# Two output stores moved up in ScalarE's queue, in a pre-norm attention and mixture-of-experts block

## The chip, the cores and the metric

The kernel runs on one core of a Trainium2 chip. The metric is the device time of one execution in microseconds (us). Device times are given as the median of several executions; one further execution was recorded by the hardware profiler.

## The reference, cut to what matters

The input is 16 sequences of 256 tokens with 128 features (4096 tokens in all, float32).

```
x = x + linear_attention(layernorm(x))            # 16 heads, elu + 1 features
x = x + moe(layernorm(x)) + shared(layernorm(x))  # 16 experts, top 2, sigmoid gates
moe(z)    = sum over the 2 chosen experts of gate * down_e(silu(gate_e z) * up_e z)
shared(z) = down(silu(z @ sg) * (z @ su))         # hidden size 256
```

The output is the last x. In the kernel it is called X1: it holds x after attention, and the shared expert's output and both routed experts' outputs are added to it in place before it is stored.

## The kernel before, in words

Tokens are worked on in 8 quads of 512 tokens, or in 16 halves of 256 (a half is half of a quad). The kernel has three stages. The first does attention, the second layer norm and the routing for each quad, and scatters the normalised rows to a buffer in HBM sorted by expert. The second loops over 80 items of 128 sorted rows, runs each through its expert and scatters the result to `results` in HBM; the shared expert's work for halves 0 to 10 lies in and before this loop. The third stage, the tail, begins when the last item is done. It is written out without a loop, as one fixed list of instructions for each engine:

- SyncE (SP) waits for the last scatters and then issues ten loads of `results` into ZB (the loads `YL`, lines 368 and 370): quads 0 to 5 whole, 512 KB each, then halves 12 to 15, 256 KB each. Each has a semaphore of its own.
- TensorE (PE) does the shared expert's gate and up matmuls of halves 11 to 15 (`shared_gu`, line 1005) and its down matmuls (`shared_d`, line 1015). The gate matmuls of a half wait for VectorE's product of two halves before.
- ScalarE (ACT) does one silu for each of these halves (`shared`, line 508). Behind the last silu it issues the ten stores of the output (`out_v`): quads 0 to 5, 256 KB each (line 546), each behind a wait for that quad's sums (`c_out`), then halves 12 to 15, 128 KB each (line 549). Its queue is in order: an instruction behind a wait stays there until the wait is met. Its last instruction waits until all stores have landed (`s_out`).
- VectorE (DVE) multiplies silu and up (`shared_h`, line 849), adds the down output to X1 (`shared_add`, line 854), and adds the two experts' results to X1 (`total(q)` for a quad, lines 958 and 960; `total_half(i)` for a half, lines 967 and 969). The second of these two adds releases `c_out`.

The order on VectorE comes from a small table, `DUE = {3: (0,), 2: (1,), 1: (2, 3)}`, read at `HALVES - i`: total(0) stands behind the product of half 13, total(1) behind that of half 14, total(2) and total(3) behind that of half 15, and then total(4), total(5), the last shared_add and the four total_half. `HALVES` is 16, `WHOLE` is 6, and `AFTER`, the first half of the tail, is 11.

Of the kernel before, what the change touches and what calls it, by code (L numbers as in the profile page):

```python
# [20 lines left out]
SPQ = QTOK // SEQ  # L21
# [13 lines left out]
HALVES = TOKENS // HALF  # L35
# [7 lines left out]
WHOLE = 6  # L43
FIRST = 2
DONE_FIRST = 16
DUE = {3: (0,), 2: (1,), 1: (2, 3)}
# [28 lines left out]
def preln_block(nc, x, w_att, bo, w_ffn, consts, tokid, out):  # L75
# [15 lines left out]
    out_v = out.rearrange("(q b p j) c -> q p b (j c)", b=SPQ, p=P, j=2)  # L91

    with ExitStack() as ctx:
        def sb(name, shape, dt=F32):
            return ctx.enter_context(nc.sbuf_tensor(name, shape, dt))
# [4 lines left out]
        def sem(name):  # L100
            return ctx.enter_context(nc.semaphore(name))
# [7 lines left out]
        X1 = sb("X1", [P, NQ * QTOK])  # L109
# [167 lines left out]
        c_sum, c_out, s_out = sem("c_sum"), sem("c_out"), sem("s_out")  # L277
# [6 lines left out]
        def quad(t, q):  # L284
            return t[:, bass.ds(q * QTOK, QTOK)]
# [120 lines left out]
        def _(act):  # L406
# [97 lines left out]
            def shared(i):  # L504

                act.wait_ge(h_gu, count_of(i) + 1)
                wait(act, h_h, count_of(i) - 1)
                nc.scalar.activation(sh_s[place(i)], banks_of(i)[0], ACT.Silu).then_inc(h_silu, 1)
# [28 lines left out]
                    silu(ITEMS - 1, BODY - 1)  # L537


            for i in range(AFTER, HALVES):  # L540
                shared(i)


            for q in range(WHOLE):
                act.wait_ge(c_out, q + 1)
                act.dma_start(out_v[q], quad(X1, q).rearrange("p (b f) -> p b f", b=SPQ)).then_inc(s_out, 16)
            for i in range(2 * WHOLE, HALVES):
                act.wait_ge(c_out, i - WHOLE + 1)
                act.dma_start(out_v[i // 2, :, i % 2, :], X1[:, i * HALF:(i + 1) * HALF]).then_inc(s_out, 16)
# [804 lines left out]
```

## Time and profile before

| | |
|---|---|
| device time, median of 3 runs | 315.89 us (313.11, 315.89, 319.8) |
| device time of the profiled execution | 313.39 us |
| span of the profiled execution, first to last instruction | 311.5 us |
| granted TensorE clock, mean of the span | 0.893 |
| tail, from the last item's last VectorE operation to the end | 285.6 to 311.5 us |
| busy in the span: PE, DVE, ACT, POOL | 77%, 52%, 41%, 39% |

Positions are microseconds from the start of the span. The profiled execution's device time is 1.9 us longer than its span. An engine name with a q (ACTq, SPq) marks what the engine's instruction queue does itself, such as issuing a transfer; the duration of such a row is that of the issue, and the time from issue to landing is given apart.

### The profile page before, as it was taken

Reading aid. Unit: us, or ns where it says so; the run is one execution under the profiler, and the core shown is the slowest. Engines: PE = TensorE matmul, PEld = TensorE weight load, DVE = VectorE, ACT = ScalarE, POOL = GpSimd, SP = SyncE. Lnnn points to the kernel's source line nnn. Section 1 sums busy time; section 2 is a strip of 40 time slices with the busy share of each in tenths; the row PEclk is TensorE's granted clock in tenths of the full one; section 3 lists DMA queues with packets and bytes.
Section 4 is the critical chain, followed back from the end, with each engine's and each line's share of the span. In section 5 each row is a group of like instructions: output and inputs, shape, how many; then the busy total and the mean of one; then the engine's idle time right before and its main releaser. Section 6 shows DMA issues by size and latency. Waiting matters only on the chain.

```text
span 311.5 us, 5386 instructions
## 1 busy us (share of the span) xinstructions
PE 238.9 (77%) x1334; PEld 189.6 (61%) x1335; DVE 163.4 (52%) x759; ACT 126.6 (41%) x341; POOL 122.9 (39%) x132
## 2 busy tenths in 40 slices
PE   6999974779486859677988678777887967886960
PEld 2477753667365647335787666666776856764850
DVE  4778975364737462524444443453454444443496
ACT  2968771646361612140024444343444344341210
POOL 0000073717272727274400465446344444655000
PEclk9999997859687968796799999999799799996995
DMA  8999930101010101013923233232233232111794
GB/s 246 432 224 221 320 114 18 51 17 45 27 51 17 54 27 52 17 51 95 121 50 90 79 99 97 70 85 77 61 87 81 68 85 77 42 42 36 265 383 169
DMA packets 26842, 33.06 MB, mean 106 GB/s; under 512 B 4531, under 2 KB 21046, under 8 KB 26694
## 3 DMA queue, kind: packets, MB, share of 16 engines
q1 hardware_dynamic: 18934, 21.16, 23.9%
q0 software_dynamic: 4096, 8.46, 8.6%
q10 hardware_dynamic: 3792, 3.21, 4.1%
q8 instruction: 8, 0.13, 0.2%
q14 instruction: 12, 0.10, 0.1%
HBM read 15.74 MB, written 12.75 MB: 91 GB/s over the span
## 4 chain that ended last, share of the span: by engine, by line
PE 64%; issue 16%; DVE 9%; ACT 5%; another core or an unknown queue 4%; DMA 1%; DVEq 0%; ACTq 0%
PE pQ L1189 6%; PE pZ L1189 6%; PE pKVN L1045 6%; PE pN L1197 3%; PE pKVN L1197 3%; PE pN L1005 3%; PE pKVN L1005 3%; PE pKV L1015 3%; PE pT L1183 3%; PE pN L1096 3%; PE pN L1061 2%; PE pKV L1035 2%; PE pKVN L1204 2%; PE pZ L1079 2%
## 5 line engine op out<-in xcount | busy, mean ns | idle before, releaser
L383 POOL DMA_INDIRECT routed<-ZB,ROWS x64 | 61.5, 961 | 91.1 <-DVE ROWS L711 74.0
L400 POOL DMA_INDIRECT results<-Y x64 | 61.3, 957 | 73.4 <-DVE Y L843 54.0
L838 DVE SCALAR_TENSOR_TENSOR Y<-pN,XS,Y 128x128 f32 x40 | 14.0, 351 | 32.6 <-PE pN L1197 10.1
L838 DVE SCALAR_TENSOR_TENSOR Y<-pKVN,XS,Y 128x128 f32 x40 | 14.0, 351 | 31.2 <-PE pKVN L1197 10.4
L1189 PE MATMUL pQ<-WF,attT 128*128 x80 | 26.3, 411 | 4.9 <-ACT attT L498 3.3
L1189 PE MATMUL pZ<-WF,attT 128*128 x80 | 26.7, 416 | 3.1 <-issue 2.9
L498 ACT COPY attT<-pT 128x256 f32<-128x256 f32 (+1 forms) x42 | 15.2, 363 | 29.1 <-PE pT L1183 11.2
L498 ACT COPY attT<-pN 128x256 f32<-128x256 f32 (+1 forms) x41 | 15.1, 368 | 24.5 <-PE pN L1183 13.4
L1045 PE MATMUL pKVN<-WA,XNT 128*128 128x256 f32 x64 | 22.3, 509 | 0.0
L1105 PE MATMUL pZ<-chosen,tri 128*128 128x64 bf16 x8 | 1.6, 200 | 23.1 <-issue 22.7
L1045 PEld LDWEIGHTS pKVN<-WA,XNT 128*128 128x128 f32 x64 | 15.8, 258 | 3.4 <-ACT XNT L441 0.5
L1197 PEld LDWEIGHTS pKVN<-WF,attT 128*128 128x128 f32 x80 | 15.9, 200 | 2.3
L1197 PEld LDWEIGHTS pN<-WF,attT 128*128 128x128 f32 x80 | 15.8, 199 | 2.5 <-issue 0.2
L1189 PEld LDWEIGHTS pQ<-WF,attT 128*128 128x128 f32 x80 | 12.5, 196 | 7.0 <-issue 6.6
L655 DVE MAX8 top<-pZ 128x8 f32<-128x16 f32 x32 | 3.4, 169 | 25.3 <-remote 20.2
L1105 PEld LDWEIGHTS pZ<-chosen,tri 128*128 128x128 bf16 x8 | 0.8, 100 | 25.3 <-issue 25.3
L1197 PE MATMUL pKVN<-WF,attT 128*128 x80 | 16.2, 286 | 0.0
L1197 PE MATMUL pN<-WF,attT 128*128 x80 | 16.2, 285 | 0.0
L1183 PE MATMUL pT<-CN,att 128*128 128x128 f32 x40 | 11.7, 293 | 5.8 <-DVE att L830 5.8
L1183 PE MATMUL pN<-CN,att 128*128 128x128 f32 x40 | 11.6, 290 | 5.5 <-DVE att L830 3.8
L1180 PE MATMUL pT<-CN,XS 128*128 128x128 f32 x40 | 11.3, 282 | 5.8 <-issue 5.8
L1189 PEld LDWEIGHTS pZ<-WF,attT 128*128 128x128 f32 x80 | 12.3, 193 | 5.1 <-issue 4.5
(192 smaller groups left out, 569.8 us busy)
## 6 DMA issues: line engine op xcount, KB each, us to landing
XS<-routed SPq DMA_DIRECT2D x80, 65.0 KB
Y<-pad SPq DMA_DIRECT2D x1, 4160.0 KB
WF<-w_ffn SPq DMA_DIRECT2D x1, 3456.0 KB, 14.5
ZB<-results SPq DMA_DIRECT2D x6, 512.0 KB, 6.0
X<-x SPq DMA_DIRECT2D x8, 256.0 KB, 5.7
routed<-pad SPq DMA_DIRECT2D x25, 65.0 KB, 13.2
out<-X ACTq DMA_DIRECT2D x6, 256.0 KB, 2.2
routed<-ZB,ROWS POOLq DMA_INDIRECT x64
```

The lines of the kernel that those rows point to most:

```text
L383: nc.gpsimd.indirect_dma_start(routed, bass.IndirectOffsetOnAxis(ap=ROWS[:, q, t, k:k + 1], axis=0), Z[:, q, t, k, :], None).then_inc(scat ...
L400: nc.gpsimd.indirect_dma_start(results, bass.IndirectOffsetOnAxis(ap=Y[:, b * YROW + D:b * YROW + D + 1].bitcast(U32), axis=0), Y[:, b * Y ...
L498: nc.scalar.copy(xhT[:, j % 2, a:b, :], pXH[j % 2][:, a:b, :]).then_inc(s_xhT, 1)
L838: nc.vector.scalar_tensor_tensor(part, pY[j % 2], XS[:, j, D + 1:D + 2], part, ALU.mult, ALU.add).then_inc(s_y, 1)
L1005: l = nc.tensor.matmul(bank[:, f * HALF:(f + 1) * HALF], WF[:, w0 + f * P:w0 + (f + 1) * P], ZT[:, bass.ds(i * HALF, HALF)], start=True, s ...
L1015: l = nc.tensor.matmul(down_bank(i)[:, t * D:(t + 1) * D], sh_h[place(i)][:, f * HALF + t * P:f * HALF + (t + 1) * P], WF[:, F_SD + f * D: ...
L1045: i = nc.tensor.matmul(pKVN[:, t, :], XNT[:, q % 2, t * P:(t + 1) * P], WA[:, W_KV:W_KV + 2 * D], start=True, stop=True)
L1096: i = nc.tensor.matmul(pO[:, t * P:(t + 1) * P], attT[:, t * P:(t + 1) * P], WA[:, W_O:W_O + D], start=False, stop=(t == QUAD - 1))
L1180: i = nc.tensor.transpose(pXH[j % 2][:, 0, :], XS[:, j, 0:D], ident)
L1183: i = nc.tensor.transpose(pXH[j % 2][:, 1, :], h[:, (j - 3) % 2, :], ident)
L1189: nc.tensor.matmul(pGU[j % 2][:, 0:2 * EXP_DIM], xhT[:, j % 2, 0, :], WF[:, bass.ds(w, 2 * EXP_DIM)], start=True, stop=True).then_inc(s_gu, 1)
L1197: nc.tensor.matmul(pY[j % 2], xhT[:, (j + 3) % 2, 1, :], WF[:, 2 * EXP_DIM:][:, bass.ds(w, D)], start=True, stop=True).then_inc(s_D, 1)
```

## The change

The six stores of whole quads become a function `store(q)`. In the loop over the last silus, after the silu of half i, ScalarE now issues the stores that the same table names at `HALVES - i + 1`: for i = 14 the store of quad 0, for i = 15 that of quad 1. Those not yet issued follow behind the loop, as before. Each store keeps its wait for `c_out`, its size and its place among the stores. The number of instructions is the same; the only pair whose order changes is the store of quad 0 (with its wait) and the silu of half 15.

```diff
+            def store(q):
+                act.wait_ge(c_out, q + 1)
+                act.dma_start(out_v[q], quad(X1, q).rearrange("p (b f) -> p b f", b=SPQ)).then_inc(s_out, 16)
+
+            stored = 0
             for i in range(AFTER, HALVES):
                 shared(i)
-
-
-            for q in range(WHOLE):
-                act.wait_ge(c_out, q + 1)
-                act.dma_start(out_v[q], quad(X1, q).rearrange("p (b f) -> p b f", b=SPQ)).then_inc(s_out, 16)
+                for q in DUE.get(HALVES - i + 1, ()):
+                    store(q)
+                    stored = q + 1
+            for q in range(stored, WHOLE):
+                store(q)
```

## Rows read from the trace of the kernel before

**Rows 1.** Timeline, ScalarE: start, duration, line, tiles, idle before and its releaser

```profile
296.29 0.60 ACT L508 ACTIVATE rq<-pQ 128x512 f32<-128x512 f32 x1 [2.02 <-PE pN L1005]
298.91 0.60 ACT L508 ACTIVATE rk<-pKVN 128x512 f32<-128x512 f32 x1 [2.02 <-PE pN L1005]
298.91 7.37 ACTq L546 DMA_DIRECT2D out<-X  x6
307.03 2.73 ACTq L549 DMA_DIRECT2D out<-X  x4
```

**Rows 2.** Timeline, VectorE in the tail

```profile
295.95 0.69 DVE L960 TENSOR_TENSOR X<-X,ZB 128x512 f32<-128x512 f32 x1
...
297.85 0.68 DVE L958 TENSOR_TENSOR X<-X,ZB 128x512 f32<-128x512 f32 x1
...
298.57 0.69 DVE L960 TENSOR_TENSOR X<-X,ZB 128x512 f32<-128x512 f32 x1
...
299.54 0.69 DVE L849 TENSOR_TENSOR ek<-pN,rk 128x512 f32<-128x512 f32 x1 [0.27 <-ACT rk L508]
...
300.48 0.68 DVE L958 TENSOR_TENSOR X<-X,ZB 128x512 f32<-128x512 f32 x1
...
306.12 0.42 DVE L967 TENSOR_TENSOR X<-X,ZB 128x256 f32<-128x256 f32 x1
...
308.96 0.42 DVE L969 TENSOR_TENSOR X<-X,ZB 128x256 f32<-128x256 f32 x1
```

**Rows 3.** Store issues by line, ns min/median/max, then time to landing: lines 546, 549

```profile
L546 ACTq DMA_DIRECT2D out<-X x6: 377/378/482, 298.9 to 305.9; - x6
DMA to landing us min/median/max: 2.1/2.2/4.2
...
L549 ACTq DMA_DIRECT2D out<-X x4: 338/344/352, 307.0 to 309.4; - x4
DMA to landing us min/median/max: 1.7/1.7/1.7
```

**Rows 4.** Load issues by line, in the same form: lines 368, 370

```profile
L368 SPq DMA_DIRECT2D ZB<-results x6: 392/470/554, 289.0 to 291.5; - x6
DMA to landing us min/median/max: 3.9/6.0/8.1
...
L370 SPq DMA_DIRECT2D ZB<-results x4: 432/466/613, 292.1 to 293.8; - x4
DMA to landing us min/median/max: 8.2/8.4/8.5
```

**Rows 5.** Stretches of the tail: busy of each engine, PE clock, DMA share, GB/s

```profile
294.00:296.00 2.00, 2.00 (x13) 1.82 (x12) 1.67 (x4) 0.26 (x1) 0.00 (x0) 1.00 1.06 401
296.00:298.00 2.00, 2.00 (x15) 1.87 (x14) 1.73 (x4) 0.60 (x1) 0.00 (x0) 1.00 1.05 398
298.00:300.00 2.00, 1.76 (x13) 1.47 (x11) 1.69 (x3) 0.60 (x1) 0.00 (x0) 1.00 1.06 389
...
304.00:306.00 2.00, 0.00 (x0) 0.00 (x0) 1.97 (x4) 0.00 (x0) 0.00 (x0) 0.50 0.64 219
306.00:308.00 2.00, 0.00 (x0) 0.00 (x0) 1.93 (x6) 0.00 (x0) 0.00 (x0) 0.50 0.56 190
308.00:310.00 2.00, 0.00 (x0) 0.00 (x0) 1.31 (x4) 0.00 (x0) 0.00 (x0) 0.50 0.54 181
```

**Rows 6.** Timeline of the last store issue alone

```profile
309.41 0.34 ACTq L549 DMA_DIRECT2D out<-X  x1
```

## The prediction

> **What bounds the kernel now.** The change touches only ScalarE's queue in the tail, so I read the tail backwards from the end. The timeline of ScalarE and that of VectorE give the order [rows 1, 2]. The last output store is issued at 309.41 [rows 6], 0.03 us after VectorE's last add ends (308.96 + 0.42 = 309.38) [rows 2], and a store of that size takes 1.7 us to land [rows 3], which gives 311.1, with 0.4 us to the span's end at 311.5. So the end is set by VectorE's last add plus one store's landing. In front of it VectorE works without a gap worth naming from 299.54: the product of half 15, one shared_add, total(2) to total(5), one shared_add, four total_half. The reader is to see in rows 2 that the first total behind it starts at 300.48 and the first total_half at 306.12, with only adds in between. In front of 299.54 VectorE was idle for 0.27 us, released by the silu of half 15 [rows 2]. That silu waited 2.02 us for PE [rows 1]. The chain before 298.91 is thus PE's matmuls, and from there on VectorE's adds; neither is the ScalarE queue. The stretches of the tail say what the DMA engines do: they are full from 294 to 300 (share 1.05 to 1.06, 389 to 401 GB/s) and about half used from 304 on (0.54 to 0.64, 181 to 219 GB/s) [rows 5].
>
> **What the change does, part by part.**
>
> Store of quad 0. Its wait is met when total(0) ends, 295.95 + 0.69 = 296.64 [rows 2]. Before, it stood behind the silu of half 15 and was issued at 298.91 [rows 1]. Now it stands behind the silu of half 14, which starts at 296.29 [rows 1]. With the 0.03 us seen from release to issue, it goes out at about 296.67, which is 2.24 us sooner.
>
> Store of quad 1. It stays behind the silu of half 15, and its wait is met only at 298.57 + 0.69 = 299.26 [rows 2]. It moves by nothing. Neither do the stores of quads 2 to 5 and the four halves, which follow total(2) and later: each waits for VectorE. So of the "first two quads" one really moves.
>
> The silu of half 15. It now has one wait and one store issue ahead of it. The issue takes 0.377 to 0.482 us on ScalarE's queue [rows 3], and the longest transfer issue of the tail took 0.613 us, on SyncE [rows 4]. With the longest, the queue is free again at 296.67 + 0.61 = 297.28, while PE releases the silu at 298.91. Cost 0; 1.63 us of PE's work is left as cover. If that cover were gone the price would be the whole issue, 0.38 to 0.61 us, since VectorE waits for this silu. The trace has no store issued between two silus of the tail. From below I take 0 (nothing is taken off the silu's path), from above 0.61; the value taken is 0, since the idle time of 2.02 us in front of the silu is a row of this very place.
>
> The added wait for total(0). Behind it on ScalarE stand the silu of half 15, and behind that the later stores; VectorE's product of half 15 waits for the silu. In the profile the wait is met 2.27 us before the silu could start. If total(0) came late by some x (its load landed late), VectorE itself would be late by x in all that follows, because it is in order: its product of half 15 would come at 299.54 + x, while the silu would end at 296.67 + 0.48 + 0.60 + x = 297.75 + x at the soonest. The wait then is never the last. Cost 0 for any x.
>
> The DMA queues. 256 KB of stores now share the engines with SyncE's loads 2.24 us sooner. At the 398 GB/s of that stretch [rows 5], 262144 bytes are 0.66 us of all engines, so each load still under way can land up to 0.66 us later. Loads of quads 0 to 5 were issued from 289.0 to 291.5 and took 3.9 us (first) to 8.1 us (last), so the last of them landed at 299.6; the four halves, issued from 292.1 to 293.8, landed by 293.8 + 8.5 = 302.3 [rows 4]. Total(2), the first total yet to come that needs a quad not in use before, starts at 300.48, and the first total_half at 306.12 [rows 2]. Even with 0.66 us more all six quads are there by 300.3 and the last half by 303.0: at least 0.2 us spare for quad 5, if total(2) needed it, and in truth 4 us, since total(5) is three totals further on. Total(1), at 297.85, needs the second load, issued right after the first, and was not waiting. Cost 0, at most 0.66 if the cover were gone.
>
> Here a rule of the Trainium skill speaks against the change. Its page "DMA: Bandwidth & Descriptors", section "Queues, rings and completion order", says that each DMA engine goes round-robin between the queues it has work for, packet by packet. By it the moved store takes up to half of each engine from SyncE's loads until it is through. This trace shows only that the store issued at 298.91 or the one behind it took up to 4.2 us, against 2.1 for one on emptier queues [rows 3], which fits sharing. By the rule or without it the sum is the same, unless a load were the last wait.
>
> The end. The last store's landing was 1.7 us for each of the four half stores, least and most alike [rows 3], with the DMA engines at 0.54 [rows 5]. The moved store has landed long before, in both kernels: before at 298.91 + 4.2 = 303.1 at the latest. So nothing is taken from the end. Bounds: -0.4 (the difference between the quads' 2.1 and the halves' 1.7, as a measure of what load can do to a landing) to 0; I take 0.
>
> Sum against the profiled execution: 313.39 + 0 + 0 + 0 + 0 = 313.4 us. Bounds of the unknown costs: 313.39 - 0.4 = 313.0 and 313.39 + 0.61 + 0.66 = 314.7. The profiled execution lies 2.5 us below the median of the three runs, and the runs reach from 313.11 to 319.8, which is more than any term above. Of the four executions known the middle is (313.39 + 315.89) / 2 = 314.6; the stated median is 315.89. I take a value between the two, 315.3, for the median of the changed kernel: no change, told on the scale of the runs.
>
> **Rivals.**
>
> 1. Back pressure on the issue (slower). If an issue on ScalarE had to wait until the DMA queues drained, the silu of half 15 would stand behind it until the loads are in, at 302.3 instead of 298.91: 3.4 us later, and VectorE in order behind it, so all of its chain to the end. That gives 313.39 + 3.4 = 316.8 on the profiled scale (1.1% more), 318.7 on that of the runs. It decides only from an issue of 298.91 - 296.67 = 2.24 us on. Against it: the two stores issued from 298.91 on met the same full engines and took 0.48 us at most [rows 3, 5], and SyncE's issues 0.61 [rows 4]. For it: nothing but that the place is new. Chance 0.04.
>
> 2. The store counts more than the adds (faster). If the tail of the output traffic, not VectorE, held the end, 256 KB off it would give up to 0.66 us plus the 2.1 against 1.7 above, so about 313.39 - 1.1 = 312.3, 314.2 on the scale of the runs. For it: the engines still carry 181 GB/s at the end [rows 5]. Against it: the half stores' landings are all alike at 1.7, so none stood behind another. Chance 0.05.
>
> 3. The change doesn't do what it says: the store of quad 0 doesn't move either, for its wait is met later than the silu of half 15. Then nothing moves at all, and the time is again 315.3. Against it: 296.64 stands 2.27 us before 298.91 [rows 1, 2]. Chance 0.03, with no effect on the time.
>
> The forecast, one store 2.2 us sooner and no change in time, has 0.88.
>
> **How the numbers follow.** The three runs span 2.1%, so about 2% is what a measurement of this kernel can tell from no change. Every case above lies within 2%: even rival 1 is at 1.1%. What puts a result outside is the spread of the runs alone; I give that 0.04 on the fast side and 0.05 on the slow side (rival 1 adds to it). So faster 0.04, same 0.91, slower 0.05. The range must hold the medians that such runs give: downwards near the fastest run, 313.11, less 0.4 for the bound at the end, so 312.7; upwards 315.89 + 0.61 + 0.66 = 317.2 by the unknown costs, and rival 1 at 318.7, which I take in because the runs themselves reach 319.8. Range 312.7 to 318.7.
>
> **What the changed profile would show.** The first issue of the quads' store line at 296.6 to 296.8 instead of 298.91, and a gap to the second at about 299.3. The silu of half 15 still at 298.9, its idle time before still about 2.0 us and still laid to PE. VectorE's product of half 15 with 0.27 us idle before it, its adds gapless to the end, the last store issued 0.03 us after the last add and landing in 1.7 us. The loads' times to landing up to 0.66 us longer for those issued last. The first store's landing time is open, and the DMA engines carry slightly more at 297 to 299 and less at 301 to 303. I would be wrong if the idle time ahead of the silu shrank to nothing with the store's issue named behind it, if a total waited for a load, or if positions ahead of 285, where no instruction is changed, came to differ by more than the tail does: then a difference would be that of the runs and not of the edit.

## The result, and the profile after

The changed kernel took 314.75 us in the median of 20 executions (311.6 to 318.95), the kernel before 314.37 us in the median of 20 (311.12 to 319.8). The stated ratio of the two, which leaves some of the longest executions out on both sides, is 1.0072, with a 95% interval of 1.0037 to 1.0108: within 2%, but to the slow side and clear of 1 by its own interval. The mean over all 20 against all 20 is 315.01 against 314.79, a ratio of 1.0007. The first question of the experiments is therefore whether the 0.7% is the edit's.

The profiled execution of the changed kernel took 311.65 us (span 309.8 us), 1.7 us less than that of the kernel before. Most lines stand five further down in the changed kernel: L958 is now L963, L849 is L854, and the moved store's line is L542.

ScalarE's timeline in the tail of the changed kernel, against [rows 1]:

```profile
294.55 0.60 ACT L508 ACTIVATE rq<-pQ 128x512 f32<-128x512 f32 x1 [2.02 <-PE pN L1010]
294.94 0.41 ACTq L542 DMA_DIRECT2D out<-X  x1
297.17 0.60 ACT L508 ACTIVATE rk<-pKVN 128x512 f32<-128x512 f32 x1 [2.02 <-PE pN L1010]
297.55 6.99 ACTq L542 DMA_DIRECT2D out<-X  x5
305.28 2.73 ACTq L554 DMA_DIRECT2D out<-X  x4
```

The store of quad 0 now stands 0.39 us behind the start of the silu of half 14 and 2.23 us ahead of that of half 15. The silu of half 15 has the same 2.02 us of idle time and the same releaser, PE, as before.

VectorE's timeline in the same stretch, against [rows 2]:

```profile
294.21 0.69 DVE L965 TENSOR_TENSOR X<-X,ZB 128x512 f32<-128x512 f32 x1
...
297.80 0.69 DVE L854 TENSOR_TENSOR ek<-pN,rk 128x512 f32<-128x512 f32 x1 [0.28 <-ACT rk L508]
...
298.73 0.68 DVE L963 TENSOR_TENSOR X<-X,ZB 128x512 f32<-128x512 f32 x1
...
307.21 0.42 DVE L974 TENSOR_TENSOR X<-X,ZB 128x256 f32<-128x256 f32 x1
```

From the start of the silu of half 15 to the end of the last add is 307.63 - 297.17 = 10.46 us; before it was 309.38 - 298.91 = 10.47 [rows 1, 2]. From the silu to the span's end is 309.8 - 297.17 = 12.6 us in both.

Issues by line of the changed kernel, stores and then the last four loads (ns min/median/max, first and last start; then us to landing), against [rows 3, 4]:

```profile
L542 ACTq DMA_DIRECT2D out<-X x6: 378/379/405, 294.9 to 304.2; - x6
DMA to landing us min/median/max: 2.1/2.1/5.6
...
L554 ACTq DMA_DIRECT2D out<-X x4: 338/345/351, 305.3 to 307.7; - x4
DMA to landing us min/median/max: 1.7/1.7/1.7
...
L370 SPq DMA_DIRECT2D ZB<-results x4: 440/456/505, 290.0 to 291.5; - x4
DMA to landing us min/median/max: 7.9/8.2/8.7
```

What is new is the 5.6 us of the moved store. It was issued 2.2 us sooner against the silu of half 15, but landed at 294.94 + 5.6 = 300.5, which is 3.4 us behind that silu; before it was 4.0 us behind. So 2.2 us of earlier issue gave 0.6 us of earlier landing, and nobody waits for either. The last half stores land in 1.7 us as before.

Is anything longer ahead of that? The tail's first shared matmul starts at 285.59 in the kernel before and 283.45 in the changed one, and from there to the silu of half 15 it takes 13.3 and 13.7 us. The difference lies where the clock rises; the first matmuls of the tail, timeline of TensorE of the changed kernel:

```profile
286.17 1.06 PE L1010 MATMUL pN<-ZT,WF 128*128 128x256 f32 x2
287.02 0.95 PE L1010 MATMUL pQ<-ZT,WF 128*128 128x256 f32 x2
287.81 0.59 PE L1010 MATMUL pN<-ZT,WF 128*128 128x256 f32 x2
```

A pair takes 1.06 us at granted clock 0.5 (1.2 GHz) and 0.59 at 1.0 (2.4 GHz), and the pair in which it changes over is the fifth of the tail here (0.95 us) and the fourth (0.98 us) in the kernel before. In two later profiles of the kernel before it was the sixth and the seventh, so this moves without any edit. The two profiles thus show no place for 2 us of loss: the tail up to that silu is 0.4 us longer by the clock, and from there on it is the same. What differs more is the time ahead of the tail, where no instruction was changed (2.14 us here, in the changed kernel's favour); by the last test that the prediction names, such a difference is one of the runs and not of the edit.

### The profile page after: what moved, and what is told of

Same layout as the page of the kernel before. It is cut to its first block, busy times and chain, and to the rows that moved or that the text cites. A ratio compares the mean times of both kernels' runs of the same rounds, so it can differ in the third digit from the quotient of the medians.

```text
span 309.8 us, 5386 instructions
## 1 busy us (share of the span) xinstructions
PE 238.1 (77%) x1334; PEld 188.6 (61%) x1335; DVE 162.8 (53%) x759; ACT 126.8 (41%) x341; POOL 122.9 (40%) x132
## 4 chain that ended last, share of the span: by engine, by line
PE 68%; issue 15%; DVE 8%; ACT 4%; another core or an unknown queue 4%; DVEq 1%; ACTq 0%
PE pQ L1194 7%; PE pKVN L1050 6%; PE pZ L1194 6%; PE pKVN L1202 4%; PE pN L1202 4%; PE pZ L994 3%; PE pN L1010 3%; PE pKVN L1010 3%; PE pKV L1020 3%; PE pN L1101 3%; PE pN L1066 2%; PE pKV L1040 2%; PE pKVN L1209 2%; PE pN L1188 2%
## 5 line engine op out<-in xcount | busy, mean ns | idle before, releaser
L1194 PE MATMUL pZ<-WF,attT 128*128 x80 | 25.9, 406 | 0.9 <-issue 0.5
L1188 PE MATMUL pN<-CN,att 128*128 128x128 f32 x40 | 11.5, 287 | 10.0 <-DVE att L835 7.5
L502 ACT ACTIVATE att<-pZ 128x128 f32<-128x128 f32 x40 | 11.2, 280 | 9.6 <-PE pQ L1194 2.8
L502 ACT ACTIVATE att<-pQ 128x128 f32<-128x128 f32 x40 | 11.1, 279 | 9.2 <-PE pQ L1194 4.1
## 6 DMA issues: line engine op xcount, KB each, us to landing
routed<-pad SPq DMA_DIRECT2D x25, 65.0 KB, 12.9
```

The source lines that it names most:

```text
L502: nc.scalar.activation(sg[:, j % 2, :], pGU[j % 2][:, 0:EXP_DIM], ACT.Silu).then_inc(s_silu, 1)
L1188: i = nc.tensor.transpose(pXH[j % 2][:, 1, :], h[:, (j - 3) % 2, :], ident)
L1194: nc.tensor.matmul(pGU[j % 2][:, 0:2 * EXP_DIM], xhT[:, j % 2, 0, :], WF[:, bass.ds(w, 2 * EXP_DIM)], start=True, stop=True).then_inc(s_gu, 1)
```

## The experiments

They ran in four sessions, on chips 0, 13, 2 and 13, each with runs of the kernel before beside them: the first four below, the next three, the next two, the last two. Its median was 319.5, 319.2, 241.6 and 314.1 us in these. Times are compared only within a session; across sessions I compare stretches of the tail.

**The kernel before against itself (no edit).**

> The kernel before, unchanged, timed against itself. Theory A (the edit costs nothing; a ratio of 1.007 between two such kernels is within what repeated runs of one kernel give): a ratio that lies within 1% of 1 and may well lie beyond its own interval, and a tail (first shared matmul of half 11 to the span's end) of 25.9 to 26.4 us. Theory B (the edit really costs some 0.7%): the ratio of this kernel against itself lies within 0.3% of 1.

Median 319.31 against 319.45 us, ratio 1.0007 (0.9969 to 1.0044). By itself that fits both theories. From the silu of half 15 (303.81) to the span's end (316.4) 12.6 us. The tail as a whole took 316.4 - 289.94 = 26.5 us, just over the 25.9 to 26.4 expected; the clock rose in its sixth pair of matmuls.

**The changed kernel a second time (no edit to it).**

> The changed kernel again. Theory A: a ratio within 1% of 1, on either side, with no steady sign; the tail again 25.9 to 26.4 us, the silu of half 15 released by PE after 2.0 us of idle time. Theory B: 1.004 to 1.011 again, and more than 1 us that can be found at one place of its trace and at no place of the kernel before.

Median 318.95 us, ratio 0.9958 (0.9922 to 0.9994), in the same session and against the same runs. This interval lies wholly below 1, as the first lay wholly above. Its ScalarE timeline:

```profile
301.97 0.60 ACT L508 ACTIVATE rq<-pQ 128x512 f32<-128x512 f32 x1 [2.02 <-PE pN L1010]
302.36 0.41 ACTq L542 DMA_DIRECT2D out<-X  x1
304.59 0.60 ACT L508 ACTIVATE rk<-pKVN 128x512 f32<-128x512 f32 x1 [2.02 <-PE pN L1010]
```

From the silu of half 13 on the tail has the same steps to 0.02 us, and 317.2 - 304.59 = 12.6 us to the end. The tail as a whole took 317.2 - 290.50 = 26.7 us, 0.3 more than expected, and here too the clock rose in the sixth pair only. Theory B's steady 0.7% falls here.

**The store of quad 0 cut in 16 (the issue, sixteen times; the same bytes).**

```diff
+                if q == 0:
+                    for g in range(8):
+                        for b in range(SPQ):
+                            act.dma_start(out_v[q, g * 16:(g + 1) * 16, b, :],
+                                          X1[g * 16:(g + 1) * 16, b * HALF:(b + 1) * HALF]).then_inc(s_out, 16)
+                    return
```

> The changed kernel with the store of quad 0 cut in 16 stores of 16 KB at the same place, between the silus of halves 14 and 15: 16 issues instead of one, same bytes. My account of the cover (the queue has 2.24 us from total(0) to PE's release of the silu of half 15, and an issue costs about 0.35 us): 16 x 0.35 = 5.6 us, so the silu of half 15 starts about 5.6 - 2.24 = 3.4 us later than PE releases it, and VectorE's last add and the span's end come 3.4 us less 0.3 us later: tail 29.0 us, time 1.0% over before. Back pressure rival (an issue waits for full queues): over 8 us for the 16. If issues are free behind the silu: no change of the tail.

Median 324.03 us, ratio 1.0158 (1.0121 to 1.0195). ScalarE's timeline of this kernel:

```profile
299.90 0.60 ACT L508 ACTIVATE rq<-pQ 128x512 f32<-128x512 f32 x1 [2.02 <-PE pN L1016]
300.30 7.45 ACTq L545 DMA_DIRECT2D out<-X  x16
307.85 0.60 ACT L508 ACTIVATE rk<-pKVN 128x512 f32<-128x512 f32 x1 [7.34 <-issue]
```

and VectorE's:

```profile
308.48 0.69 DVE L860 TENSOR_TENSOR ek<-pN,rk 128x512 f32<-128x512 f32 x1 [5.59 <-ACT rk L508]
```

The silu of half 15 now waits for the queue ("issue") and no more for PE. With the usual 2.62 us from one silu to the next it would have come at 302.52; it came 5.33 us later, and VectorE's idle time ahead of its product grew by the same (5.59 against 0.27). The stretch from the silu to the end stayed 320.5 - 307.85 = 12.65 us, and the time went up by 5.0 us (1.58% of 319.45). So this is the path, and the cover is real: 7.45 us of issues cost 5.3, and the first 2.1 us were free. My 3.4 us were too little because 16 issues took 7.45 us and not 5.6, 0.47 us from one to the next. The lines for two stretches of the sixteen show whether the full DMA engines made them dear:

```profile
L545 ACTq DMA_DIRECT2D out<-X x9: 360/442/443, 300.3 to 304.0; - x9
L545 ACTq DMA_DIRECT2D out<-X x4: 442/442/462, 305.9 to 307.3; - x4
```

They did not. From 300 to 306 the DMA engines were full (share 1.05 to 1.06), from 306.2 to 307.75 they were mostly idle (0.28), and an issue took 0.44 us in both. The first of the sixteen, with none right ahead of it, took 0.36. So the dearer price goes with standing right behind another issue.

**2 MB more behind the moved store (the traffic, not the issue).**

```diff
+                if q == 0:
+                    act.dma_start(spare, ZT[:, :]).then_inc(s_out, 16)
```

> The changed kernel with one more store of 2 MB (all of ZT to a spare buffer in HBM, which the output does not need) issued right behind the store of quad 0: one more issue, eight times the bytes moved early. My account (DMA traffic placed early has about 4 us of cover in front of the totals): 2 MB at 390 GB/s are 5.4 us of all engines; the last quad load lands at up to 305.0 and the last half at up to 307.7, measured as in the kernel before, against use at 304.5 and 308.5, so VectorE loses 0 to 1.5 us, and the output's own stores pile up and end up to 1 us later: tail 26.5 to 28.5 us, 0.2 to 0.8% over before. If the traffic already costs in the changed kernel (0.7% for 256 KB), this one is over 3% slower.

Median 320.32 us, ratio 1.0039 (1.0007 to 1.0072). Issues of this kernel, the last four loads and the last four stores:

```profile
L371 SPq DMA_DIRECT2D ZB<-results x4: 432/456/467, 297.2 to 298.6; - x4
DMA to landing us min/median/max: 8.0/8.5/11.5
```

```profile
L557 ACTq DMA_DIRECT2D out<-X x4: 351/540/839, 311.7 to 314.2; - x4
DMA to landing us min/median/max: 3.6/4.2/4.9
```

The silu of half 15 kept its 2.02 us of idle time, and VectorE's chain its 10.5 us (303.58 to 314.05): the last load, up to 11.5 us under way, was in at 310.1 and used at 313.18. The loss sits behind VectorE: stores that landed in 1.7 us now take 3.6 and more, and 318.2 - 303.58 = 14.6 us from the silu to the end, 2.0 more than before. Eight times the moved bytes thus cost 2.0 us in the profile and 0.4% in the timing. They cost it at the end: from 311 to 317 the DMA engines were full (share 0.92 to 1.08) with these bytes and the quads' stores behind them, just when the last stores came. The 256 KB of the change were in 7 us before VectorE's last add (300.5 against 307.6).

**The changed kernel a third time.**

> The changed kernel a third time. Theory A (no cost; single ratios of this kernel scatter by about 0.5%): a ratio between 0.994 and 1.008 with either sign, and again 12.6 us from the start of the silu of half 15 to the span's end, 2.62 us from the silu before it. Theory B (a real cost of 0.7% that the second timing missed by chance): 1.004 or more, with a stretch of the trace that is longer than in both profiles of the kernel before.

Ratio 1.0041 (1.0009 to 1.0074), 2.62 us between the two last silus, 316.9 - 304.23 = 12.7 us to the end. The number is to the slow side again; no stretch of the tail is longer. It does not decide by itself.

**All quad stores held until total(5) is done.**

```diff
             for q in range(WHOLE):
-                act.wait_ge(c_out, q + 1)
+                act.wait_ge(c_out, WHOLE)
```

> The other way round: the kernel before with the six quad stores all held until total(5) is done, so 1.5 MB of stores start 7.0 us (first) to 0 us (last) later. My account (stores are off the path as long as what is queued is through before the last store): from about 306 on 2 MB of stores at 390 GB/s are 5.4 us of the DMA engines, so they end near 311.4 plus about 1.5 for the last landing = 312.9 against 311.1 on the scale of the kernel before: 1.8 us at the end, from the silu of half 15 to the span's end 14.4 us instead of 12.6, VectorE unchanged. If the time of storing is of no matter: 12.6 us.

Ratio 1.0081 (1.0042 to 1.0121); 318.3 - 303.38 = 14.9 us from the silu to the end. ScalarE's queue in the timeline of this kernel:

```profile
310.36 3.52 ACTq L546 DMA_DIRECT2D out<-X  x6
313.92 2.44 ACTq L549 DMA_DIRECT2D out<-X  x4
```

VectorE's last add ends at 313.84, 10.46 us behind the silu as ever, but the last of the ten issues starts only at 315.9. The size came out roughly (2.3 us against 1.8), the cause only half: I had put it on the DMA engines, and of the 2.3 us some 2.0 are the queue's ten issues, 0.6 us each, that ran on behind VectorE; the landings of the half stores were 2.0 to 2.9 us. The issues grew from 0.41 us to 0.73 on the way, with the DMA engines full from 312 to 316 (share 1.03 and 1.01). Whether the stores already queued made them grow, no run tells. So the placing of stores does matter once several pile up at the end. The first one was never among those that do.

**total(4) and total(5) on GpSimd.**

```diff
+            for q in (4, 5):                    # GpSimd, behind the last scatter
+                pool.wait_ge(yl[q], 16)
+                pool.wait_ge(h_add, last_count(2 * q + 1) + 1)
+                x1 = quad(X1, q).rearrange("p (t c) -> p t c", t=QUAD)
+                nc.gpsimd.tensor_tensor(x1, x1, y_of[:, q, :, 0, :], ALU.add).then_inc(p_sum, 1)
+                pool.wait_ge(p_sum, q - 3)
+                nc.gpsimd.tensor_tensor(x1, x1, y_of[:, q, :, 1, :], ALU.add).then_inc(p_out, 1)
...
-            total(4)                            # VectorE
-            total(5)
```

> The kernel before with total(4) and total(5), four adds of 128x512 float32, given to GpSimd, which is idle in the tail. My account (VectorE's adds are what sets the end, and their four take 2.65 us): last add, last store and span's end 2.65 us sooner, 9.95 us from the silu of half 15 to the end, ratio 0.992, as long as GpSimd takes under 1.9 us for each add (its quads have landed by about 299.6, and their stores are due by 307). If the end is set by stores or the DMA queues and not by VectorE: 12.6 us stay. If GpSimd's adds slow VectorE's down by sharing, VectorE's adds take more than 0.69 us in that stretch.

Ratio 1.0025 (0.9987 to 1.0063). GpSimd's and VectorE's timelines of this kernel:

```profile
304.34 1.81 POOL L411 TENSOR_TENSOR X<-X,ZB 128x512 f32<-128x512 f32 x1
306.12 1.71 POOL L409 TENSOR_TENSOR X<-X,ZB 128x512 f32<-128x512 f32 x1
...
305.07 1.64 DVE L972 TENSOR_TENSOR X<-X,ZB 128x512 f32<-128x512 f32 x1
306.63 1.74 DVE L970 TENSOR_TENSOR X<-X,ZB 128x512 f32<-128x512 f32 x1
```

VectorE's adds take 1.63 to 1.74 us where they took 0.69. Three of them lost 2.9 us, more than the four saved ones were worth (2.65), and the stretch from the silu (302.78) to the end grew to 13.5 us, where I had expected 9.95. Of the 0.9 us more, VectorE's chain has 0.3. The other 0.6 lie behind the last landing (313.57 + 1.7 = 315.3, against an end at 316.3; in the kernel before the end comes 0.4 us behind the last landing); what fills them wasn't tested. The Trainium skill has this in "SBUF — State Buffer", section "Who interferes with whom": a VectorE instruction with two inputs in SBUF contends with a GpSimd instruction that reads SBUF, over a shared pair of ports that works as an exclusive lock. The trace agrees: the GpSimd add begun at 304.34 ran until 306.15, so a VectorE add of 0.69 us that came at 305.07 and waited for it would take 1.77 us in all, and it took 1.64.

**total(4) and total(5) on TensorE and ScalarE.**

```diff
+            def sums(q):                        # TensorE
+                ...
+                nc.tensor.matmul(bank[:, :], ident, quad(X1, q), start=True, stop=False)
+                nc.tensor.matmul(bank[:, :], ident, y_of[:, q, :, 0, :], start=False, stop=False)
+                nc.tensor.matmul(bank[:, :], ident, y_of[:, q, :, 1, :], start=False, stop=True).then_inc(p_tot, 1)
+            def copy(q):                        # ScalarE
+                act.wait_ge(p_tot, q - 3)
+                nc.scalar.copy(quad(X1, q), (pT, pZ)[q - 4][:, :]).then_inc(a_tot, 1)
```

> The kernel before with the sums of quads 4 and 5 taken from VectorE and given to TensorE (three matmuls with the identity for each quad: X1 and the two expert results, added up in a free PSUM bank) and to ScalarE (one copy of 512 columns back to X1). My account (VectorE's chain of adds sets the end, GpSimd failed only because its adds and VectorE's slowed each other): VectorE's four adds, 2.65 us, are gone with no slowing, the last add and the last store come 2.65 us sooner, 9.95 us from the silu of half 15 to the span's end, ratio 0.992. TensorE needs 3 x 0.86 us for each quad: quad 4 before the down matmuls of half 15, quad 5 behind them, done some 7.5 us after the silu of half 15, ahead of the last add at 7.8. If the output traffic sets the end once VectorE is faster: 10.5 to 12.6 us. If ScalarE's stores and copies hold each other up: a last store issued more than 0.1 us behind the last add.

Ratio 1.0000 (0.9962 to 1.0037), in the session at 241 us; 238.5 - 225.62 = 12.9 us from the silu to the end. Its timeline shows my mistake:

```profile
228.17 1.12 PE L1323 MATMUL pT<-X,CN 128*128 128x512 f32 x2 [1.70 <-DMA ZB<-results]
...
231.94 0.42 DVE L876 TENSOR_TENSOR X<-pKVN,X 128x256 f32<-128x256 f32 x1 [2.00 <-PE pKVN L1035]
```

The sums of quad 4 stood ahead of the down matmuls of half 15 and waited 1.70 us for their load, and VectorE then waited 2.00 us for those down matmuls. The wait removed from one engine had come back on another. VectorE's last add still came 0.5 us sooner behind the silu than in the kernel before (235.54 - 225.62 = 9.9 us against 10.5). That gained nothing, since ScalarE's queue issued its last store only at 236.1, 0.5 us behind that add.

**The changed kernel a fourth time, in that session.**

> The changed kernel a fourth time, for the size of the scatter. Theory A: a ratio between 0.994 and 1.008, the mean of the four within 0.4% of 1, and 12.6 us from the silu of half 15 to the end, 2.62 us between the two last silus. Theory B: above 1.004.

Median 241.38 against 241.57 us, ratio 1.0014 (0.9979 to 1.0049). It also tried the case that I had worked out on paper, a total(0) that comes late:

```profile
223.79 0.69 DVE L963 TENSOR_TENSOR X<-X,ZB 128x512 f32<-128x512 f32 x1 [0.72 <-DMA ZB<-results]
...
225.24 0.41 ACTq L542 DMA_DIRECT2D out<-X  x1
...
226.66 0.60 ACT L508 ACTIVATE rk<-pKVN 128x512 f32<-128x512 f32 x1 [2.02 <-PE pN L1010]
```

total(0) waited 0.72 us for its load, so the store went out only 1.42 us ahead of the silu of half 15, and that silu still waited 2.02 us for PE. 12.7 us to the end; the 0.1 us over the other sessions is VectorE's, which was behind from its wait for the load and went without a gap from there to its last add.

**The same totals, behind the down matmuls of half 15.** The edit is shown against the run with TensorE's totals above; on ScalarE the store of quad 3 also moves ahead of the copy of quad 4.

```diff
-                if i == HALVES - 1:
-                    sums(4)
                 shared_d(i, 1 if i == HALVES - 1 else 0)
...
+            sums(4)
             sums(5)
```

> The kernel before with the sums of quads 4 and 5 on TensorE and ScalarE, as in the run with TensorE's totals, but both behind the down matmuls of half 15, so that a late load of quad 4 can't hold those up, and the store of quad 3 ahead of the copy of quad 4. My account: VectorE's 2.65 us of adds are gone and its 2.00 us wait for the down matmuls of half 15 too. From the silu of half 15: TensorE's sums of quad 5 are done at about 7.6 us, its copy at 8.2, the last add at 7.9, the last store at about 9.2, the end 11.0 instead of 12.6 us on a chip where the DMA queues leave room; with 6.3 MB of loads and stores at 385 GB/s (16.4 us) and about 1.7 for the last landing, the end can't come before about 18 us from the first load, against 18.8 measured on the full-clock chip and 21.4 on the other. So 0.8 to 1.6 us less, ratio 0.995 to 0.998. If something else sets the end: 12.6 to 12.9 us.

Ratio 0.9927 (0.986 to 0.9994), medians 314.4 and 314.1. 309.4 - 297.77 = 11.6 us from the silu to the end, 1.0 less than in every run of the two kernels, but not the 11.0 us that I expected. The tail is faster by what its trace says, 0.3%. The device time gains less: it is 2.2 us longer than the span in this kernel and in the two others that declare two more semaphores (GpSimd's and TensorE's totals), and 1.9 in all the rest. The cause of that wasn't tested; what is left is some 0.6 us, or 0.2%, and the mean over all executions is in line with it (313.61 against 314.35, ratio 0.9977). The medians do not show it. The stated 0.9927 is beyond the 0.995 to 0.998 expected, and a stated ratio of this size is not proof here, as the changed kernel's own first one shows. ScalarE's queue now sets the end:

```profile
305.49 0.58 ACT L554 COPY X<-pZ 128x512 f32<-128x512 f32 x1 [1.99 <-PE pZ L1325]
306.11 0.39 ACTq L550 DMA_DIRECT2D out<-X  x1
306.54 0.98 ACTq L558 DMA_DIRECT2D out<-X  x2
```

VectorE's last add ends at 305.57, and the last store is issued at about 307.1.

**The kernel before against itself, once more.**

> The kernel before against itself once more. Theory A: a ratio between 0.994 and 1.006; 12.6 to 12.8 us from the silu of half 15 to the end, as in the changed kernel.

Ratio 1.0041 (0.9994 to 1.0088), for two kernels that are the same. 310.2 - 297.61 = 12.6 us to the end.

## Why the prediction came out as it did

**The time.** The four stated ratios of the changed kernel are 1.0072, 0.9958, 1.0041 and 1.0014, mean 1.0021; the two of the kernel before against itself are 1.0007 and 1.0041, mean 1.0024. The first two intervals of the changed kernel do not even overlap, so a single interval here is narrower than what a repeat gives. Taken over all executions of each comparison, the ratios of the means are 1.0007, 0.9986, 1.0020 and 0.9994 for the changed kernel, mean 1.0002, and 1.0010 and 1.0021 for the kernel before against itself. So most of the 0.7% is gone when every execution counts. The measured 314.75 us lies in the range of 312.7 to 318.7, near the 315.3 forecast. But the forecast was no change, and the first comparison moved by 0.7%, beyond its interval, to the slow side. The step that failed is the one on what a measurement of this kernel can tell: I took the 2.1% spread of three single runs for it ("about 2% is what a measurement of this kernel can tell from no change"), while the comparison has an interval of 0.35% to either side; and I had given no case by which it could lie clear of 1 with nothing in the tail changed. What the runs showed in its place: the sign did not hold, and the kernel before against itself gave 1.0041 too. An effect of some 0.3% in either direction isn't excluded by these ratios. The traces exclude it behind the last silu to 0.1 us (0.03%): VectorE's last add starts 10.03 to 10.05 us behind that silu in all three profiles of the kernel before and in three of the changed one, and 10.12 in the fourth, with the late load. What differs between executions of one kernel lies ahead: in the three profiles of the kernel before that silu starts at 297.6, 298.9 and 303.8. Why the first comparison came out at 1.0072 remains open.

**The end of the chain.** Right: VectorE's last add and one landing of 1.7 us, with 12.6 us from the last silu to the end in all three profiles of the kernel before, and 12.6 to 12.7 in all four of the changed one. The 1.7 us by which the changed kernel's profiled execution was the shorter came ahead of the tail, which began 2.1 us sooner.

**One store moves, by 2.24 us.** Right, and only one: 2.23 us ahead of the silu of half 15, the second at 297.55. I had it 0.38 us behind the silu of half 14's start (296.67 against 296.29); it was 0.39.

**The silu of half 15 is covered.** Right: 2.02 us of idle time, laid to PE, in all of its profiles. The sixteenfold issue showed from where on it is not. The price beyond that, 0.35 us for each issue in what I expected of that run, was undersized: right behind one another they took 0.47 us each, with full DMA engines and with nearly idle ones. The prediction's 0.38 to 0.61 for a single issue held (0.41).

**The added wait.** Right, and seen with a late total(0) in the session at 241 us.

**The DMA queues.** No term for the time, right; the last loads took 8.7 us against 8.5 (bound 0.66 more). Two details were off. I wrote that the moved store would have landed long before; it took 5.6 us against 4.0 and landed 0.6 us sooner against the silu, not 2.2. And I read the long landing as sharing, by the rule of the Trainium skill in "DMA: Bandwidth & Descriptors", section "Queues, rings and completion order", that engines take queues in turn, packet by packet. The packets in the traces say otherwise for most of that time. q1 carries SyncE's loads and q10 ScalarE's stores (packets, MB, share of the 16 engines). First the changed kernel from the store's issue on, 294.94 to 298.5; then its profile in the session at 241 us, 225.24 to 228.8 and 229.5 to 234.0:

```profile
q1 hardware_dynamic: 742, 1.38, 105.4%
...
q1 hardware_dynamic: 693, 1.34, 103.5%
...
q1 hardware_dynamic: 652, 1.20, 70.5%
q10 hardware_dynamic: 598, 0.58, 36.6%
```

In the first two stretches the store has not one packet. So it did not share the engines in that time; it had not begun. Its first packet moves 3.7 to 3.8 us behind its issue in all four profiles of the changed kernel. For the first store of the kernel before, issued when the loads were nearly through, it is 1.3 to 2.3 us (301.25 against 298.91 in the first profile), and in the run with the stores held, where nothing else was under way, 0.9 us. Once both queues move packets, in the last two lines, they go nearly one for one (652 against 598), as that rule says, and since a packet of the loads has about twice the bytes, the stores get a third of them. No run shows what holds the first packet back. It explains why 2.2 us of earlier issue gave only 0.6 us of earlier landing, and nobody waited for it.

**The rivals.** Back pressure did not occur at one issue (0.41 us). Issues did lengthen where many stores were queued, to 0.73 us among the ten held stores and to 0.84 us behind the 2 MB. That the stores' queue counts more than the adds is wrong for this store, and right for ten at once and for 2 MB more.

## What to carry to other kernels

Ask of a moved store who waits for it: here the last add and one landing set the end, and a store issued 12 us before that can neither help nor, as long as its issue fits into the wait of the next instruction on the queue, hurt. Find the room for it in the trace (the idle time ahead of the next instruction, less the time until the store's own wait is met) and price several issues by those that stand right behind another (0.44 us here, against 0.34 to 0.41 for one by itself). And time a kernel against itself before explaining a difference below 1%: here the kernel before against itself gave up to 1.0041, and the same change gave 1.0072 and 0.9958.

## What the runs showed of the hardware that was not expected

- The sessions differ more than any edit: the kernel before took 314, 319 and 241 us. The last was on a chip of its own (2), but 314 and 319 us are also the medians of two sessions on one chip (13). In the session at 241 us the profiles of two kernels have a granted clock of 0.978 and 0.996 over the span, where all others have 0.87 to 0.91.
- Issues of small stores on ScalarE took 0.47 us from one to the next (16 in 7.45 us), with full and with nearly idle DMA engines alike, and up to 0.84 us with 2 MB queued ahead, against 0.34 us for one by itself at the end.
- A store issued while SyncE's loads keep the DMA engines full moved its first packet only 3.7 to 3.8 us behind its issue, against 0.9 us with no other transfer under way.
- A float32 add of 128x512 with both inputs in SBUF took VectorE 0.69 us alone and 1.63 to 1.74 us beside one on GpSimd, which took 1.5 to 1.8 us itself.
